# A two-layer latent attention network on one core: the heads' outputs scaled by ScalarE, one activation per head, and the statistics of the context rows placed anew

## The chip, the cores and the metric

The kernel runs on 1 core of one Trainium2 chip. The metric is the device time of one execution in microseconds (us), as a median of runs: 2179.64 us of 3 (2179.64 to 2184.43).

## The reference

`x` is 16 batches of 64 latents of width 128, `ctx` 16 batches of 1601 context rows of width 128. Six blocks add to `x`, one after the other: a cross attention (16 heads of 64), a selective scan, a small attention with a mixture of experts, a second cross attention (with a mask over the context), a state space block, and a feed-forward block with 4-bit quantization. The change touches the two cross attentions, which are, cut to what matters:

```python
xn = layer_norm(ctx); lat = layer_norm(x)
q = lat @ Wq
kv = concatenate([xn, lat], axis=1) @ Wkv            # 1601 + 64 rows
logits = einsum('bhld,bhsd->bhls', q * scale, k * scale)
w = softmax(logits, axis=-1)                         # in the second one masked
out = einsum('bhls,bhsd->bhld', w, v)
x = x + out.transpose(0, 2, 1, 3).reshape(b, 64, 1024) @ Wo
```

The kernel never makes k and v: the head weights are folded into the queries (`qk_hi`, `qk_lo`) and into an output matrix per head (`vo_c` for context rows, `vo_l` for latents), and a column of ones yields the softmax's sum.

## The kernel before, in words

One function, `cross_attention` (L120), prepares weights and calls `attention_loop` (L497), once unmasked (the first loop) and once masked (the second loop). The loop goes over the 16 batches, in pairs: `par` is 0 for the first batch of a pair and 1 for the second. One batch is called a half (of a pair). The engines run their own programs, and meet only through semaphores. Pair 0, pair 6 and pair 7 are written out; pairs 1 to 5 are five trips of a hardware loop (`Fori`, L665), so that each engine jumps back four times per attention, at the end of a `par` 1 half.

A half is 28 steps u (26 for 13 tiles of 128 context rows by two groups of 8 heads, 2 for the latents). In step u:

- TensorE (L875 on) makes the scores of step u + 3 (three matmuls, L786 to L788), into a ring of 4 PSUM banks, then the products of step u with the context rows (three matmuls, L805 to L807), then the side items of the step. Scores of u + 3 need the ring place that `p_lo` of step u - 1 frees. In the last steps the first scores of the next half are made: two of them in step 26, one in step 27. Before the products of step 26 it waits until the bank pair `aux` is free.
- ScalarE (L936 on) makes two exponentials of each score tile: `p_hi` in fp16 (L929), then the same in fp32 in place (L930). After these of step u it works on the side items of step u - 1 (`LAG` is 1). At the end of a half it copies the sums out of PSUM (L943), once the products of step 25 are done, and then takes the next half's step 0.
- VectorE (L1129 on) makes `p_lo`, the rest (L1134), then parts of the statistics of context rows (first loop only), then the side items of step u - 1. In step 1 it copies the latents' sums of the half before out of `aux` (L1099).
- GpSimd normalizes context rows (L264) and splits them into fp16 halves (L221, L223) in the first loop, splits queries of the second batch of a pair (L962, L952, at the end of a `par` 1 half), and adds up the heads' outputs (`add_heads`, L709).
- SyncE issues the DMAs: rows that carry the maxima (L729, L731), raw context rows (L179 on), stores and transposed loads.

Side items share the PSUM bank pair `aux`, so each waits until the one before is read (semaphore `aux_free`). `items` (L572) places them: 16 `max` items (the row maxima of the next batch's scores) and a `turn` in each half, four `q` items at the start of a `par` 1 half, and in a `par` 0 half three `out` items at steps 20, 21 and 22: outputs of the pair before for 6, 6 and 4 heads, each head two fp32 matmuls of 129 columns (L812, L813). VectorE's `project` (L1101) takes an `out` item: reciprocals of the sums (L1113, two instructions of 3 heads), then products of outputs and reciprocals (L1119, two instructions), which free `aux`. Seven `par` 0 halves of each attention have `out` items (all but the first).

The statistics (`context_stats`, L227) of one batch are 13 `bn_stats` (L236), an aggregation of five small instructions (L243 to L249), an addition (L253) and nine dependent steps of a reciprocal square root. Before, those for batch b + 2 run in half b: four `bn_stats` in each of steps 0 to 2, one in step 3, the rest in steps 3 to 8. GpSimd's L264 waits for them.

Of the kernel before, what the change touches and what calls it, by code (L numbers as in the profile page):

```python
# [14 lines left out]
ACT = mybir.ActivationFunctionType  # L15
# [3 lines left out]
B, L, D = 16, 64, 128  # L19
# [45 lines left out]
STATS_PARTS = 4 + 2 + RSQRT_STEPS  # L65
# [54 lines left out]
def cross_attention(nc, glob, name, ctx_dram, mask_dram, w_dram):  # L120
# [12 lines left out]
    with ExitStack() as st:  # L133
# [93 lines left out]
        def context_stats(v, wait, n, par, i, part):  # L227


            if part == 0:  # L230
                x_step[0] = Steps(v, norm_steps, n * NORM_STEPS)
                v.wait_ge(raw_in[par], (i + 1) * 48)
            steps = x_step[0]
            if part < 4:
                for j in range(4 * part, min(4 * part + 4, KT)):
                    steps.mark(v.bn_stats(xstats[:, j, :], raw[par][:, j, :]))  # L236
            elif part == 4:
# [12 lines left out]
            else:  # L250
                steps.wait()
                if part == 5:
                    steps.mark(v.tensor_scalar(xrv[:, :], xvar[:, :], LN_EPS, None, ALU.add))  # L253
                else:
                    steps.mark(rsqrt_step(v, part - 6, xr[:, :], xrv[:, :], xrt[:, :]))
# [16 lines left out]
        with ExitStack() as pre:  # L272
# [53 lines left out]
            def copy_of(n, made):  # L326
# [6 lines left out]
                (VF_C, 0, range(0, 4)), (VF_L, 0, range(4, 8)), (K_C, 0, range(8, STATS_PARTS)), (VO + 2, 1, range(0, 4)))}  # L333
# [163 lines left out]
def attention_loop(nc, glob, name, st, sb, sem, psum, held, mask_dram, context_stats, context_normal):  # L497
# [74 lines left out]
    def items(par, first, last, pre=False):  # L572
# [14 lines left out]
        for item in todo:  # L587
# [3 lines left out]
            else:  # L591
                u += 1 + {paused: PAUSE[par][0], ("max", 2 * NC_ - 1): PAUSE[par][1]}.get(item, 0)
# [118 lines left out]
    with nc.Block() as block:  # L711
        @block.sync
        def _(sp):
# [32 lines left out]
            def body(at):  # L746
# [3 lines left out]
                if at.has_next:  # L750
                    rows(at)
                if at.has_next3 and not masked:
                    sp.wait_ge(xt_ready, at.b + 2)
                    load_raw(sp, at.b + 3, at.npar, at.ni + 1)
                if at.has_next2:
# [288 lines left out]
        def _(v):  # L1044
            def stats_parts(u):

                if u < 4:
                    return (u,), (4,) if u == 3 else ()
                parts = [k for k in (2 * u - 3, 2 * u - 2) if k < STATS_PARTS]
                return parts[:1], parts[1:]  # L1050
# [50 lines left out]
            def project(a, at, ready, pair, used=None):  # L1101
# [3 lines left out]
                if a == 0 and used is not None:  # L1105
                    v.wait_ge(later_q_used, used)
                if a == 0 and not (isinstance(pair, int) and pair == 0):
                    v.wait_ge(sum_steps, pair * SUM_STEPS)
# [5 lines left out]
                steps.wait()  # L1114
# [7 lines left out]
            def before(at):  # L1122
                for item in at.index:
                    consume(at, item)
                    if item == ("q", Q_ITEMS - 1) and not masked:
                        for part in range(4, STATS_PARTS):
                            context_stats(v, wait_alone, 1, 1, 0, part)

            def body(at):  # L1129
                for u in range(STEPS):  # L1130
# [6 lines left out]
                    soon, later = stats_parts(u) if at.has_next2 and not masked else ((), ())  # L1137
                    for part in soon:
# [1267 lines left out]
```

## Time and profile before

| what | value |
|---|---|
| median of 3 runs | 2179.64 us |
| profiled execution | 2175.95 us, its span 2174.3 us |
| TensorE busy | 2012.8 us, 93% |
| VectorE busy | 1700.0 us, 78% |
| ScalarE busy | 1284.3 us, 59% |
| first attention loop | about 90 to 906 us of the span |
| second attention loop | about 1221 to 2002 us of the span |

Busy times are shares of the whole span over stages with different limits; inside the loops the rows of the timeline tell which engine is waited for. A span of several instructions in one row ("x2") runs from the first one's start to the last one's end. An ACT or DVE instruction's shown duration overlaps with the next one's start.

### The profile page before, as it was taken

To read this page: it belongs to the slowest core of one execution; us is meant where nothing else is said; L and a number is where in the kernel's file an instruction comes from. 1 tells how busy PE (TensorE), PEld (TensorE's weight loads), DVE (VectorE), ACT (ScalarE), POOL (GpSimd) and SP (SyncE) were. 2 spreads that over 40 slices of the span, in tenths; PEclk is the share of its full clock that TensorE was granted. 3 is DMA by queue.
4 is the path that set the end of the run, shared out by engine and by line. 5 is a ranking of instruction groups with operands and counts; after the bars stand their busy time and mean duration, and the time that the engine had idled before them with its cause. 6 is when DMAs were issued, how large, how long until landed. Compare 5 with 4: busy or idle time off the path is not lost. (4 is left out here: it accounts for less than half of the span.)

```text
span 2174.3 us, 37348 instructions
## 1 busy us (share of the span) xinstructions
PE 2012.8 (93%) x11706; PEld 1090.7 (50%) x11706; DVE 1700.0 (78%) x4108; ACT 1284.3 (59%) x2308; POOL 600.7 (28%) x648
## 2 busy tenths in 40 slices
PE   5899999999999999889798999999999999999886
PEld 4444545353535455433567445454545454544584
DVE  5789797979788887589666877778787979785657
ACT  2376666666666666644323486868687777777211
POOL 3435353534343432059201102121111111110000
PEclk8899999999999999989999899999999999999897
DMA  3222222222222211033104012121111111110100
GB/s 111 81 64 64 65 64 63 64 63 63 63 64 63 91 37 48 9 95 126 48 1 110 5 37 52 31 61 36 35 36 36 36 36 37 36 33 1 27 2 10
DMA packets 148169, 108.91 MB, mean 50 GB/s; under 512 B 120748, under 2 KB 136088, under 8 KB 148024
## 3 DMA queue, kind: packets, MB, share of 16 engines
q1 hardware_dynamic: 148024, 107.26, 17.2%
q8 instruction: 57, 0.93, 0.2%
q14 instruction: 88, 0.72, 0.1%
HBM read 65.15 MB, written 14.29 MB: 37 GB/s over the span
## 5 line engine op out<-in xcount | busy, mean ns | idle before, releaser
L1134 DVE TENSOR_TENSOR x_p_lo<-x_psum,x_p_hi 128x512 f16<-128x512 f32 (+2 forms) x896 | 605.5, 684 | 153.8 <-ACT x_psum L930 141.1
L929 ACT ACTIVATE x_p_hi<-x_psum 128x512 f16<-128x512 f32 (+2 forms) x480 | 287.4, 599 | 303.3 <-PE x_psum L788 301.5
L929 ACT ACTIVATE x_p_hi<-x_psum,x_bcol 128x512 f16<-128x512 f32 (+1 forms) x416 | 288.8, 694 | 139.6 <-PE x_psum L788 137.4
L805 PE MATMUL x_psum<-x_p_hi,x_x_both 128*128 128x512 f16 (+1 forms) x832 | 316.7, 381 | 33.1 <-DVE x_p_lo L1134 32.5
L786 PE MATMUL x_psum<-x_q,x_xT_both 128*128 128x512 f16 x832 | 316.9, 381 | 0.9 <-DMA x_q<-x_shift_rows 0.7
L807 PE MATMUL x_psum<-x_p_hi,x_x_both 128*128 128x512 f16 (+1 forms) x832 | 315.8, 380 | 0.0
L787 PE MATMUL x_psum<-x_q,x_xT_both 128*128 128x512 f16 x832 | 315.8, 380 | 0.0
L806 PE MATMUL x_psum<-x_p_lo,x_x_both 128*128 128x512 f16 (+1 forms) x832 | 315.8, 380 | 0.0
L788 PE MATMUL x_psum<-x_q,x_xT_both 128*128 128x512 f16 x832 | 315.8, 380 | 0.0
L1073 DVE CUSTOM_DVE_ANT_0 x_junk<-x_psum,x_brow 128x512 bf16<-128x512 f32 (+2 forms) x512 | 279.7, 585 | 9.9 <-PE x_psum L852 9.2
L930 ACT ACTIVATE x_psum<-x_psum 128x512 f32<-128x512 f32 (+2 forms) x480 | 286.0, 596 | 0.6
L852 PE MATMUL x_psum<-x_xT_both,x_q 128*128 128x512 f16 (+2 forms) x1024 | 268.9, 340 | 15.0 <-DVE x_mx L1076 3.9
L1076 DVE TENSOR_REDUCE x_mx<-x_psum 128x1 f32<-128x512 f32 (+2 forms) x512 | 276.5, 585 | 6.9 <-PE x_psum L852 6.4
L930 ACT ACTIVATE x_psum<-x_psum,x_bcol 128x512 f32<-128x512 f32 (+1 forms) x416 | 276.2, 664 | 0.2
L264 POOL TENSOR_SCALAR x_xt<-x_raw,x_xmean,x_xr 128x127 f32<-128x127 f32 x208 | 166.5, 816 | 298.1 <-DVE x_xr L85 298.1
L852 PEld LDWEIGHTS x_psum<-x_xT_both,x_q 128*128 128x128 f16 x1024 | 99.0, 97 | 186.7 <-DVE x_mx L1076 48.6
L979 POOL TENSOR_SCALAR x_brow<-x_mrow 128x1536 bf16<-128x1536 uint8 x16 | 36.3, 2266 | 531.6 <-DVE x_shift_rows L1095 479.2
L805 PEld LDWEIGHTS x_psum<-x_p_hi,x_x_both 128*128 128x128 f16 (+1 forms) x832 | 81.0, 97 | 171.7 <-DVE x_p_lo L1134 85.3
L709 POOL TENSOR_TENSOR x_prod<-x_prod 128x1024 f32<-128x1024 f32 (+3 forms) x56 | 67.0, 1197 | 237.1 <-DVE x_prod L1119 233.8
L788 PEld LDWEIGHTS x_psum<-x_q,x_xT_both 128*128 128x128 f16 x832 | 81.4, 98 | 98.6 <-issue 0.3
L807 PEld LDWEIGHTS x_psum<-x_p_hi,x_x_both 128*128 128x128 f16 (+1 forms) x832 | 81.4, 98 | 98.4 <-issue 0.3
L806 PEld LDWEIGHTS x_psum<-x_p_lo,x_x_both 128*128 128x128 f16 (+1 forms) x832 | 81.5, 98 | 79.5 <-issue 0.3
(450 smaller groups left out, 3256.9 us busy)
## 6 DMA issues: line engine op xcount, KB each, us to landing
x_x_both<-context_rows SPq DMA_DIRECT2D x32, 832.0 KB, 5.4
context_rows<-x_x SPq DMA_DIRECT2D x16, 832.0 KB, 5.7
x_raw<-in_ctx SPq DMA_DIRECT2D x16, 768.0 KB
ssm_c_row<-ssm_bc_rows SPq DMA_DIRECT2D x16, 512.0 KB, 4.1
ssm_b_wide<-ssm_bc_rows SPq DMA_DIRECT2D x7, 512.0 KB, 3.5
x_mrow<-in_mask_BxS_bk SPq DMA_DIRECT2D x16, 200.1 KB
x_Wkv<-in_L_xattn_Wkv SPq DMA_DIRECT2D x4, 512.0 KB, 4.9
x_xT_both<-context_rows SPq DMA_TRANSPOSE x96, 3.7
```

Source lines behind the costliest of these rows:

```text
L786: pe.matmul(out, k_hi, q_hi[s][par][:, chunks, :], start=True, stop=False)
L787: pe.matmul(out, k_hi, q_lo[s][par][:, chunks, :], start=False, stop=False)
L788: pe.matmul(out, k_lo, q_hi[s][par][:, chunks, :], start=False, stop=True).then_inc(s_ready, 1)
L805: pe.matmul(out, v_hi, p_hi[r][rows, :], start=start, stop=False)
L806: pe.matmul(out, v_hi, p_lo[r][rows, :], start=False, stop=False)
L807: pe.matmul(out, v_lo, p_hi[r][rows, :], start=False, stop=stop).then_inc(pv_done, 1)
L852: ins = pe.matmul(aux[:, 512 * bank:512 * bank + w], lhs, xT_hi[at.npar][:, k:k + w], start=True, stop=True)
L929: act.activation(p_hi[r][rows, :], score[r][rows, :], ACT.Exp, scale=SCORE_UNIT, **bias).then_inc(p_hi_ready, 1)
L930: act.activation(score[r][rows, :], score[r][rows, :], ACT.Exp, scale=SCORE_UNIT, **bias).then_inc(p32_ready, 1)
L1073: ins = v.tensor_tensor_reduce(junk[:, 512 * bank:512 * bank + w], src, brow[:, w0:w0 + w], 1.0, -3.4e38, ALU.add, ALU.max, m)
L1076: ins = v.tensor_reduce(m, src, AX.X, ALU.max)
L1134: v.tensor_tensor(p_lo[r][rows, :], score[r][rows, :], p_hi[r][rows, :], ALU.subtract).then_inc(p_lo_ready, 1)
```

## The change

It has four parts. In both loops, VectorE's `project` keeps only the reciprocals; the products move to ScalarE as one activation (copy with the reciprocal as a per-partition scale) per head, 6, 6 and 4 of them, taken as side items at step u - 1 = 20, 22 and 24. The `out` items get a free step behind the first and the second, so that they stand at steps 20, 22 and 24. In the first loop, the `bn_stats` and the aggregation for batch b + 3 run in steps 23 to 27 of half b (3, 3, 3, 2, 2 and then the aggregation), and the reciprocal square root of that batch in steps 0 to 3 of the next half (3, 2, 3, 1). The first half keeps its early statistics too. And SyncE issues the load of raw rows ahead of the maxima's rows and no longer behind them. After the loop, VectorE scales the last pair's outputs itself (`scale_last`).

```diff
+STATS_OF = ((0, 3), (3, 6), (6, 9), (9, 11), (11, KT))
+AGGR = len(STATS_OF)
+ROOTS = AGGR + 2
+STATS_PARTS = ROOTS + RSQRT_STEPS
...
-                u += 1 + {paused: PAUSE[par][0], ("max", 2 * NC_ - 1): PAUSE[par][1]}.get(item, 0)
+                u += 1 + {paused: PAUSE[par][0], ("max", 2 * NC_ - 1): PAUSE[par][1], ("out", 0): 1, ("out", 1): 1}.get(item, 0)
...
-                if at.has_next:
-                    rows(at)
                 if at.has_next3 and not masked:
                     sp.wait_ge(xt_ready, at.b + 2)
                     load_raw(sp, at.b + 3, at.npar, at.ni + 1)
+                if at.has_next:
+                    rows(at)
...
                 kind, a = item
+                if kind == "out":
+
+                    if a == 0:
+                        act.wait_ge(later_q_used, LATER_PARTS * (at.i + 1))
+                    act.wait_ge(out_steps, (at.i - 1) * OUT_STEPS + 2 * (a + 1))
+                    for j, h in enumerate(out_heads(a)):
+                        ins = act.activation(prod[:, h, :], out_place(j, aux)[:, 0:D], ACT.Copy, scale=rec[:, h:h + 1])
+                    ins.then_inc(aux_free, 2)
+                    return
...
-            def stats_parts(u):
-
-                if u < 4:
-                    return (u,), (4,) if u == 3 else ()
-                parts = [k for k in (2 * u - 3, 2 * u - 2) if k < STATS_PARTS]
-                return parts[:1], parts[1:]
+            def stats_parts(u, at):
+
+                if at.first and at.par == 0:
+                    early = [[k] for k in range(AGGR)] + [[AGGR, AGGR + 1]]
+                    early += [[k, k + 1, k + 2] for k in range(ROOTS, STATS_PARTS, 3)]
+                else:
+                    early = [[ROOTS, ROOTS + 1, ROOTS + 2], [ROOTS + 3, ROOTS + 4], [ROOTS + 5, ROOTS + 6, ROOTS + 7], [ROOTS + 8]]
+                late = {LAST - AGGR + 1 + k: [k] for k in range(AGGR)}
+                late[LAST] += [AGGR, AGGR + 1]
+                return early[u] if u < len(early) else (), late.get(u, ())
...
-                steps.wait()
+
+            def scale_last(a, at):
+                v.wait_ge(out_steps, (PAIRS - 1) * OUT_STEPS + 2 * (a + 1))
+                if a == 0:
+                    v.wait_ge(sum_steps, (PAIRS - 1) * SUM_STEPS)
+                heads = out_heads(a)
                 for g in range(0, len(heads), 3):
...
-                    soon, later = stats_parts(u) if at.has_next2 and not masked else ((), ())
-                    for part in soon:
+                    two, three = stats_parts(u, at) if not masked else ((), ())
+                    for part in two if at.has_next2 else ():
                         context_stats(v, wait_alone, at.b + 2, at.par, at.i + 1, part)
                     for item in at.items.get(u - LAG, []):
                         if item[0] == "out":
-                            project(item[1], aux, at.ready(item), at.i - 1, LATER_PARTS * (at.i + 1))
+                            project(item[1], aux, at.ready(item), at.i - 1)
                         else:
                             consume(at, item)
-                    for part in later:
-                        context_stats(v, wait_alone, at.b + 2, at.par, at.i + 1, part)
+                    for part in three if at.has_next3 else ():
+                        context_stats(v, wait_alone, at.b + 3, at.npar, at.ni + 1, part)
```

## Rows read from the trace of the kernel before

**Rows 1.** The page's first part: engine, busy us, share, instructions.
```profile
PE 2012.8 (93%) x11706; PEld 1090.7 (50%) x11706; DVE 1700.0 (78%) x4108; ACT 1284.3 (59%) x2308; POOL 600.7 (28%) x648
```
**Rows 2.** Timeline of PE: start, us, line, count [idle before].
```profile
544.82 0.39 PE L812 MATMUL x_psum<-x_vo_c,x_sum_c 128*128 128x129 f32 x2
...
547.50 0.38 PE L786 MATMUL x_psum<-x_q,x_xT_both 128*128 128x512 f16 x1
...
549.26 0.49 PE L812 MATMUL x_psum<-x_vo_c,x_sum_c 128*128 128x129 f32 x2 [0.31 <-DVE x_prod L1119]
...
553.61 0.49 PE L812 MATMUL x_psum<-x_vo_c,x_sum_c 128*128 128x129 f32 x2
...
555.50 0.38 PE L786 MATMUL x_psum<-x_q,x_latTphi 128*128 128x512 f16 x1
...
564.98 0.22 PE L832 MATMUL x_psum<-x_lnT_hi,x_qk_hi 128*128 x1
...
1567.36 0.22 PE L832 MATMUL x_psum<-x_lnT_hi,x_qk_hi 128*128 x1
```
**Rows 3.** Timeline of DVE in the same `par` 0 half.
```profile
547.91 0.25 DVE L1113 RECIPROCAL x_rec<-x_psum 128x3 f32<-128x3 f32 x2 [2.29 <-PE x_psum L813]
548.19 1.02 DVE L1119 TENSOR_TENSOR x_prod<-x_psum,x_rec 128x384 f32<-128x384 f32 x2
549.13 0.68 DVE L1134 TENSOR_TENSOR x_p_lo<-x_psum,x_p_hi 128x512 f16<-128x512 f32 x1
...
561.03 0.69 DVE L1134 TENSOR_TENSOR x_p_lo<-x_psum,x_p_hi 128x512 f16<-128x512 f32 x1 [1.61 <-ACT x_psum L930]
```
**Rows 4.** Timeline of ACT in the same `par` 0 half.
```profile
542.51 0.60 ACT L929 ACTIVATE x_p_hi<-x_psum 128x512 f16<-128x512 f32 x1 [1.43 <-PE x_psum L788]
...
548.35 0.59 ACT L929 ACTIVATE x_p_hi<-x_psum 65x512 f16<-65x512 f32 x1 [2.89 <-PE x_psum L788]
548.84 0.58 ACT L930 ACTIVATE x_psum<-x_psum 65x512 f32<-65x512 f32 x1
...
558.93 1.08 ACT L943 ACTIVATE x_sum_c<-x_psum 128x512 f32<-128x512 f32 x2 [0.23 <-PE x_psum L807]
```
**Rows 5.** Groups of ACT by form: count | busy us, mean ns.
```profile
L929 ACT ACTIVATE x_p_hi<-x_psum,x_bcol 128x512 f16<-128x512 f32 x384 | 267.0, 695 | 91.8 <-PE x_psum L788 89.8
...
L929 ACT ACTIVATE x_p_hi<-x_psum 128x512 f16<-128x512 f32 x384 | 230.6, 601 | 202.3 <-PE x_psum L788 202.3
...
L2305 ACT ACTIVATE fp_hT<-fp_psum 96x128 f32<-96x128 f32 x8 | 2.1, 268 | 0.0
```
**Rows 6.** Waits: who for whom, us in total, times, longest.
```profile
PEld x_psum L812 <- DVE x_prod L1119: 18.7, 28, 0.8
```
**Rows 7.** Timeline of DVE: a jump back of the loop, a written-out boundary.
```profile
500.49 2.60 DVE L1134 TENSOR_TENSOR x_p_lo<-x_psum,x_p_hi 65x512 f16<-65x512 f32 x4
506.87 0.69 DVE L1134 TENSOR_TENSOR x_p_lo<-x_psum,x_p_hi 128x512 f16<-128x512 f32 x1 [3.78 <-ACT x_psum L930]
...
515.08 0.69 DVE L1134 TENSOR_TENSOR x_p_lo<-x_psum,x_p_hi 128x512 f16<-128x512 f32 x1
...
819.68 0.69 DVE L1134 TENSOR_TENSOR x_p_lo<-x_psum,x_p_hi 128x512 f16<-128x512 f32 x1 [1.85 <-ACT x_psum L930]
```
**Rows 8.** Groups of DVE in the half of 508 to 562 us.
```profile
L236 DVE BATCH_NORM_STATS2 x_xstats<-x_raw 128x6 f32<-128x128 f32 x13 | 2.9, 277 | 0.0
```
**Rows 9.** Line L1081: duration ns min/median/max, first and last start.
```profile
L1081 DVE TENSOR_TENSOR x_shift<-x_const_rows x32: 400/407/1802, 80.5 to 1944.2; 8x256 f32<-8x256 f16 x32
```
**Rows 10.** Timeline of DVE: L1081 in a `par` 0 half.
```profile
538.55 1.79 DVE L1081 TENSOR_TENSOR x_shift<-x_const_rows 8x256 f32<-8x256 f16 x1
```
**Rows 11.** Timeline of POOL.
```profile
503.62 4.49 POOL L952 TENSOR_TENSOR x_q<-x_prod,x_q 128x512 f16<-128x512 f32 x4
...
536.73 3.34 POOL L223 TENSOR_TENSOR x_x<-x_xt,x_x 128x1664 f16<-128x1664 f32 x1 [0.15 <-POOL x_x L221]
```

More of the change, by code:

```diff
@@ L64 @@
 NORM_STEPS = KT + 5 + 1 + RSQRT_STEPS
-STATS_PARTS = 4 + 2 + RSQRT_STEPS
+STATS_OF = ((0, 3), (3, 6), (6, 9), (9, 11), (11, KT))
+AGGR = len(STATS_OF)
+ROOTS = AGGR + 2
+STATS_PARTS = ROOTS + RSQRT_STEPS
 def rsqrt_step(v, k, out, val, t):
@@ L232, in context_stats @@
                 v.wait_ge(raw_in[par], (i + 1) * 48)
+            if part == ROOTS:
+                x_step[0] = Steps(v, norm_steps, n * NORM_STEPS)
+                x_step[0].n = KT + 5 + 1
             steps = x_step[0]
-            if part < 4:
-                for j in range(4 * part, min(4 * part + 4, KT)):
+            if part < AGGR:
+                for j in range(*STATS_OF[part]):
                     steps.mark(v.bn_stats(xstats[:, j, :], raw[par][:, j, :]))
-            elif part == 4:
+            elif part == AGGR:
                 if not (isinstance(n, int) and n == 0):
@@ L251, in context_stats @@
                 steps.wait()
-                if part == 5:
+                if part == AGGR + 1:
                     steps.mark(v.tensor_scalar(xrv[:, :], xvar[:, :], LN_EPS, None, ALU.add))
                 else:
-                    steps.mark(rsqrt_step(v, part - 6, xr[:, :], xrv[:, :], xrt[:, :]))
+                    steps.mark(rsqrt_step(v, part - ROOTS, xr[:, :], xrv[:, :], xrt[:, :]))
             assert part < STATS_PARTS - 1 or steps.n == NORM_STEPS
@@ L332, in cross_attention @@
             STATS_WITH = {n: [(b, part) for part in parts] for n, b, parts in (
-                (VF_C, 0, range(0, 4)), (VF_L, 0, range(4, 8)), (K_C, 0, range(8, STATS_PARTS)), (VO + 2, 1, range(0, 4)))}
+                (VF_C, 0, range(0, AGGR)), (VF_L, 0, range(AGGR, ROOTS + 2)), (K_C, 0, range(ROOTS + 2, STATS_PARTS)), (VO + 2, 1, range(0, AGGR)))}
             if masked:
@@ L1099, in latents_sums, with project @@
                 v.tensor_copy(sum_l[:, :, par, :], aux.rearrange("p (h l) -> p h l", l=L)).then_inc(aux_free, 2)
-            def project(a, at, ready, pair, used=None):
+            def project(a, at, ready, pair):
                 steps = Steps(v, out_steps, pair * OUT_STEPS + 2 * a)
                 v.wait_ge(aux_ready, ready)
[L1105 to L1108, printed above, removed]
                 heads = out_heads(a)
@@ L1125, in before @@
                     if item == ("q", Q_ITEMS - 1) and not masked:
-                        for part in range(4, STATS_PARTS):
+                        for part in range(AGGR, STATS_PARTS):
                             context_stats(v, wait_alone, 1, 1, 0, part)
@@ L1152, in _ @@
                 project(a, last_place(a), 2 * (k + a + 1 - B), PAIRS - 1)
+                scale_last(a, last_place(a))
             v.wait_ge(aux_free, 2 * (k + OUT_ITEMS))
```

## The prediction

> **What bounds the kernel now.** I read the page's first part, then the table of waits, then the timelines of TensorE, VectorE and ScalarE side by side over one `par` 0 half of the first loop (508 to 562 us) and one of the second, then the jump back of the loop. TensorE is busy 93% of the span, so it is the engine to feed; ScalarE with 59% looks as if it had room for more [rows 1]. In the steps with `out` items TensorE works through 12 fp32 matmuls in 2.68 us (544.82 to 547.50) for six heads and in 1.89 us (553.61 to 555.50) for four [rows 2]. VectorE and ScalarE wait there, not TensorE: VectorE 2.29 us before the reciprocals [rows 3], ScalarE 2.89 us before exponential 24 [rows 4]. TensorE waits for the scaling only before the second and third item, 18.7 us of weight loads' idle time in all, 28 times [rows 6].
>
> The reader is to see one more thing in rows 4. ScalarE ran exponential 22 at 542.51, long before the first `out` item was made. It is ahead of VectorE, and that lead is what keeps the chain short: when VectorE is done with the scaling at 549.1, `p_lo` 22 starts at once [rows 3].
>
> **Part 1, the scaling moves.** VectorE loses two products an item, six a pair: 1.02 us for an item of six heads [rows 3], some 2.8 us a pair. ScalarE gets 16 activations a pair. An activation's price here: 128 columns last 268 ns, 512 columns 601 ns, and with a per-partition pointer (the bias) 695, so 94 more [rows 5]. The trace has no 128-column one with a pointer. Two of 512 columns start 0.49 us apart (548.35, 548.84) though each lasts 0.59, so about 0.10 of each is hidden [rows 4]. My value: 0.268 + 0.094 - 0.10, 0.27 us each when back to back (an estimate), so 1.6 for six heads and 1.1 for four. Ends: 0.17 (the pointer costs nothing) and 0.36 (nothing overlaps).
>
> What counts is the order on ScalarE. It takes the item of step 20 after the exponentials of step 21, and then waits in order: exponentials 22 and 23, which it made early before, stand behind the wait for the reciprocals. VectorE's `p_lo` 22 waits for exponential 22, and TensorE's products 22 wait for `p_lo` 22. Before: reciprocals, scaling, `p_lo`. Now: reciprocals, scaling, two exponentials, `p_lo`. And the free step behind each item takes away what TensorE did meanwhile: `out` 1 ran at 549.26, ahead of products 22.
>
> I walk it in the profiled half, with: three fp16 matmuls 0.65; matmuls' end to reciprocals 0.20 (0.41 the first time) and 0.25 for them [rows 2, 3]; 0.1 to ScalarE (estimate); from the start of a pair of exponentials 1.10 to `p_lo` (0.49 + 0.58 + 0.03) and 0.98 to ScalarE's next instruction [rows 4]; `p_lo` 0.68 [rows 3].
>
> - `out` 0 ends 547.50; reciprocals until 548.16; ScalarE scales until 549.91; `p_lo` 22 at 551.01 (549.13 before). TensorE had finished products 21 and scores 25 at 549.45, and starts products 22 at 551.74: 2.3 us idle. `out` 1 runs 552.39 to 555.07.
> - Products 23 and scores 26 and 27 fill TensorE to 557.02. Reciprocals until 555.52, scaling until 557.27, exponential 24, `p_lo` 24 at 558.37, products 24 at 559.10: 2.1 us idle. `out` 2 runs 559.75 to 561.64.
> - Products 25 and two sets of next scores fill until 563.59. Scaling until 563.29, exponential 26, `p_lo` 26 at 564.39, products 26 at 565.12: 1.5 us idle. `aux` is free in time.
> - ScalarE goes on without a gap: exponential 27 at 564.27, sums' copies 1.0 [rows 4], exponential 0 of the next half at 566.23. `p_lo` 0 at 567.33, before at 561.03 [rows 3].
> - In step 1 of the next half VectorE frees `aux` (L1099) at about 570.3, and only then does TensorE start `q` 0: 570.35, before at 564.98 [rows 2].
>
> So the half gets 5.4 us longer, with TensorE's old waits for the scaling already gone from the count. In the second loop the exponentials with a bias pointer last 94 ns more [rows 5], with four such pairs in the chain, and the same walk ends 5.9 us later than the 1567.36 of before [rows 2]. From `q` 0 on TensorE is the bound in both, so I see nothing that gives it back. Seven such halves in each loop: 7 x 5.4 + 7 x 5.9 = 79 us. With 0.17 or 0.36 for an activation the chain of 16 is 1.6 shorter or 1.4 longer: 57 to 99.
>
> **Part 2, the statistics.** At the jump back VectorE is idle 3.78 us, at a boundary without one 1.85 [rows 7]. The jump follows its last instruction, and that is now later by 13 `bn_stats` (2.9 us, [rows 8], less the overlap, 2.5) and six small ones (about 1.0, an estimate from two reciprocals in 0.25, [rows 3]): 3.6 us. In the next three steps 12 `bn_stats` go (2.3) and eight roots at about 0.2 come (1.6): so the fifth `p_lo` (515.08, [rows 7]) is late by 2.9. Four jumps: +11.6. At the written-out boundaries, and at the ends of `par` 0 halves, VectorE's idle time hides the added work: 0. What is won: L1081 takes 0.41 usually and 1.8 in the `par` 0 halves of the first loop whose statistics run (one of eight such in [rows 10]; median and maximum in [rows 9]). There it ends as GpSimd's L223 ends, 536.73 + 3.34 = 540.07 [rows 11]. With the roots done at step 3 instead of 8, GpSimd is through some 8 us before, in six halves (the first keeps its early order): -6 x 1.39 = -8.3. Sum +3.3, with ends -8 (nothing lost at the jumps) and +11.6 - 8.3 + 4 x 4.5 = +21: the aggregation falls in the time of GpSimd's L952 (4.49 us, [rows 11]), and each small instruction could wait as L1081 did.
>
> The Trainium skill's GPSIMD Engine Reference, section Specifications, says that GpSimd's SBUF interface is shared with VectorE and is contended by VectorE instructions with two SBUF inputs; the long L1081 (two SBUF inputs) agrees, and by that rule the aggregation's subtraction and addition would wait too, 1 us or so per jump, which lies inside the bounds above.
>
> **Part 3, SyncE.** The raw load is issued at the start of a half instead of between the maxima's rows and the store; three issues less stand before the store, 1.6 us. VectorE is late there by more than that, so 0; ends 0 and -1.6 x 6 = -10.
>
> **Sum.** 79 + 3 = 82. The profiled execution took 2175.95, 3.7 less than the median of 2179.64. 2175.95 + 82 = 2258, against the median 2262.
>
> **The rivals.**
>
> - Faster: ScalarE's lead hides it all. If it reached the items with its exponentials done (as VectorE's did), the moved work would fall into 2.9 us of its idle time, TensorE would lose its waits before L812 in 14 halves (about -10 of the 18.7 us of [rows 6], since a weight load's idle time is partly hidden), and L1081's stall would go (-8.3): 2161. It decides at whether exponential u + 2 stands before or behind item u on ScalarE. The diff puts it behind. 7%.
> - Half of it: the activations are cheap (0.17), handovers shorter, and something later in the half absorbs 1.5 us of the shift: 14 x 3.3 = 46, about 2226. For it: the waits before L812 are short, 0.7 each [rows 6], so handovers here are quick. Against: TensorE has no idle time from `q` 0 to the `turn`. 13%.
> - More: the small VectorE instructions wait for GpSimd at jumps and also where L709 runs now, at the start of `par` 1: 2262 + 18 + 7 x 1 = 2287. 12%.
> - ScalarE's jump back. Now VectorE alone pays for it [rows 7]; with 16 more activations and their waits in a trip ScalarE could pay the same 3.8 us at 8 jumps, +30: 2292. For it, VectorE's trip is longer than ScalarE's, against it, it stays shorter after the change too. 3%. The Trainium skill (Runtime: NRT & Kernel Launch, Instruction fetch mechanics) says that a taken branch whose target is out of a two-page window waits for a fetch; VectorE's 3.78 us fit that, and of ScalarE's room no row tells.
> - The change is hidden: 5%, 2180.
>
> The forecast has 60%. A difference under 0.3% (6.5 us) could not be told from none. Faster 0.07, same 0.05, slower 0.88. Range: from 2222 to 2290, which leaves out the first and last rival and some of the fourth.
>
> **What would show it.** Right: in a `par` 0 half ScalarE is idle some 7 us behind exponential 21, until the reciprocals are there, then six activations, then L929; TensorE idle about 2.3, 2.1 and 1.5 us before L805, released by `p_lo`, and no more at L812; halves of the second loop with `out` items 6 us longer, `par` 1 halves the same; L1081 at 0.41 from the third half on; VectorE's idle time at the jump still near 3.8, but starting 3.6 later. Wrong: exponential 22 before the first scaling, or `par` 0 halves of the second loop within 1 us of their length before.

## The result, and the profile after

The changed kernel takes 2279.14 us (median of 4, 2278.13 to 2280.14) against 2180.77 for the kernel before in the same runs: 4.5% slower, ratio 1.0448 [1.043, 1.0466]. The profiled execution took 2280.1 us. Forecast: 2262, range 2222 to 2290. The measured difference is 98.4 us, the forecast one was 82.

Names after: scores L792 to L794, products L811 to L813, `out` L818 and L819, exponentials L944 and L945, ScalarE's scaling L919, reciprocals L1128, `p_lo` L1154, shift addition L1100 (was L1081), sums' copies L958 and L1118, `bn_stats` L242, aggregation L249 to L259.

The page's first part, which answers to [rows 1]: 10 us left VectorE, 53 came to ScalarE, and the span of the profiled execution grew by 104.

```profile
PE 2030.2 (89%) x11706; PEld 1106.2 (49%) x11706; DVE 1690.2 (74%) x4024; ACT 1337.0 (59%) x2532; POOL 601.7 (26%) x648
```

The page's groups (count | busy us, mean ns of one | idle time ahead of them, what ended most of it). ScalarE's 224 activations sit behind 167.5 us of waiting for reciprocals. TensorE's products have 107.3 us of idle time that `p_lo` ended. The weight loads' waits for the scaling, 18.7 us in [rows 6], are gone.

```profile
L1154 DVE TENSOR_TENSOR x_p_lo<-x_psum,x_p_hi 128x512 f16<-128x512 f32 (+2 forms) x896 | 609.1, 684 | 249.9 <-ACT x_psum L945 225.8
L811 PE MATMUL x_psum<-x_p_hi,x_x_both 128*128 128x512 f16 (+1 forms) x832 | 319.1, 384 | 108.6 <-DVE x_p_lo L1154 107.3
L919 ACT ACTIVATE x_prod<-x_psum,x_rec 128x128 f32<-128x128 f32 x224 | 62.5, 374 | 167.5 <-DVE x_rec L1128 167.5
```

The table of waits (us in total, times, longest) for TensorE's products, first of the kernel before, then of the changed one, shows where the new time went:

```profile
PE x_psum L805 <- DVE x_p_lo L1134: 32.5, 49, 1.5
```

```profile
PE x_psum L811 <- DVE x_p_lo L1154: 123.9, 92, 6.3
```

ScalarE's timeline in a `par` 0 half of the first loop (start, us, line, count [idle before]); it answers to [rows 4]. Exponential 21 ends at 457.66, and the next thing is the first item, 5.52 us later. Exponentials 22 and 23 (464.69 on) stand behind it, where before exponential 22 ran ahead of the item. The same happens before the second and the third item.

```profile
457.07 0.59 ACT L945 ACTIVATE x_psum<-x_psum 128x512 f32<-128x512 f32 x1
463.18 1.66 ACT L919 ACTIVATE x_prod<-x_psum,x_rec 128x128 f32<-128x128 f32 x6 [5.52 <-DVE x_rec L1128]
464.69 0.63 ACT L944 ACTIVATE x_p_hi<-x_psum 128x512 f16<-128x512 f32 x1
...
470.41 1.66 ACT L919 ACTIVATE x_prod<-x_psum,x_rec 128x128 f32<-128x128 f32 x6 [3.60 <-DVE x_rec L1128]
...
476.71 1.14 ACT L919 ACTIVATE x_prod<-x_psum,x_rec 128x128 f32<-128x128 f32 x4 [2.69 <-DVE x_rec L1128]
```

VectorE in the same stretch, answering to [rows 3]: from reciprocals to `p_lo` 22 it was 1.2 us (547.91 to 549.13), now it is 2.95, and VectorE is idle for 2.70 of it.

```profile
462.89 0.25 DVE L1128 RECIPROCAL x_rec<-x_psum 128x3 f32<-128x3 f32 x2 [2.08 <-PE x_psum L819]
465.84 0.69 DVE L1154 TENSOR_TENSOR x_p_lo<-x_psum,x_p_hi 128x512 f16<-128x512 f32 x1 [2.70 <-ACT x_psum L945]
```

TensorE, at products 22, 24 and 26 of that half. In the fifth half of the second loop the same three rows read 1.95, 1.92 and 1.21.

```profile
466.59 0.39 PE L811 MATMUL x_psum<-x_p_hi,x_x_both 128*128 128x512 f16 x1 [1.79 <-DVE x_p_lo L1154]
...
473.80 0.39 PE L811 MATMUL x_psum<-x_p_hi,x_x_both 65*128 65x512 f16 x1 [1.76 <-DVE x_p_lo L1154]
...
479.57 0.39 PE L811 MATMUL x_psum<-x_p_hi,x_latphi 64*128 64x512 f16 x1 [1.22 <-DVE x_p_lo L1154]
```

The second thing to see is the jump back. VectorE's timeline, answering to [rows 7]: the aggregation's L249 and L250 take 0.96 and 1.19 us (0.17 each in the kernel before, where GpSimd is idle), the last small instruction ends at 535.66, and `p_lo` 0 comes 4.29 us later, with nothing to wait for ("issue"). L249 and L250 end at 533.62 and 534.73, each as one of GpSimd's four L967 ends (533.58 and 534.70).

```profile
532.66 0.96 DVE L249 TENSOR_TENSOR x_xd<-x_xstats 128x13 f32<-128x13 f32 x1
533.54 1.19 DVE L250 TENSOR_TENSOR x_xm<-x_xstats 128x13 f32<-128x13 f32 x1
...
535.45 0.21 DVE L259 TENSOR_SCALAR x_xrv<-x_xvar 128x13 f32<-128x13 f32 x1
539.96 0.69 DVE L1154 TENSOR_TENSOR x_p_lo<-x_psum,x_p_hi 128x512 f16<-128x512 f32 x1 [4.29 <-issue]
```

GpSimd in that stretch works on the queries (as in [rows 11], 4.5 us):

```profile
530.19 4.51 POOL L967 TENSOR_TENSOR x_q<-x_prod,x_q 128x512 f16<-128x512 f32 x4
```

TensorE's first products behind the jump, of the kernel before and then of the changed one: 0.76 us idle became 6.22. At the four jumps of the first loop it is 1.22, 1.22, 0.76 and 1.24 before, and 6.29, 6.14, 6.22 and 6.21 after.

```profile
507.79 0.39 PE L805 MATMUL x_psum<-x_p_hi,x_x_both 128*128 128x512 f16 x1 [0.76 <-DVE x_p_lo L1134]
```

```profile
540.88 0.60 PE L811 MATMUL x_psum<-x_p_hi,x_x_both 128*128 128x512 f16 x1 [6.22 <-DVE x_p_lo L1154]
```

And the same jump of the changed kernel by windows (the number behind POOL's count is the granted TensorE clock, then the DMA share and GB/s). From 536 to 539 no engine works. From 539 on TensorE runs at 0.50, its 1.2 GHz level, for 6.8 us; this happens behind all four jumps (near 307, 423, 539 and 655 us). Before, windows over the same jump show 1.00 throughout, and no stretch at the lower clock follows any of the first loop's jumps.

```profile
536.00:539.00 3.00, 0.00 (x0) 0.00 (x0) 0.00 (x0) 0.00 (x0) 0.00 (x0) 1.00 1.04 229
539.00:541.00 2.00, 0.12 (x1) 0.13 (x2) 0.97 (x4) 0.00 (x0) 0.00 (x0) 0.52 0.97 319
541.00:543.00 2.00, 2.00 (x6) 0.62 (x6) 1.98 (x4) 0.00 (x0) 0.00 (x0) 0.50 0.93 376
```

What was won, answering to [rows 9]: the shift addition's longest is 1106 ns, no longer 1802. The 1106 is the one at 82.5 us, ahead of the loop. Of the seven that took 1.73 to 1.80 us in the first loop's `par` 0 halves, the first now takes 0.69 and the others 0.40.

```profile
L1100 DVE TENSOR_TENSOR x_shift<-x_const_rows x32: 402/406/1106, 82.5 to 2043.2; 8x256 f32<-8x256 f16 x32
```

### The profile page after: what moved, and what is told of

It is laid out like the page before. It is cut to its first block and busy times, and to the rows that moved or that the text cites. A ratio compares the mean times of both kernels' runs of the same rounds, so it can differ in the third digit from the quotient of the medians.

```text
span 2278.3 us, 37473 instructions
## 1 busy us (share of the span) xinstructions
PE 2030.2 (89%) x11706; PEld 1106.2 (49%) x11706; DVE 1690.2 (74%) x4024; ACT 1337.0 (59%) x2532; POOL 601.7 (26%) x648
## 5 line engine op out<-in xcount | busy, mean ns | idle before, releaser
L1154 DVE TENSOR_TENSOR x_p_lo<-x_psum,x_p_hi 128x512 f16<-128x512 f32 (+2 forms) x896 | 609.1, 684 | 249.9 <-ACT x_psum L945 225.8
L944 ACT ACTIVATE x_p_hi<-x_psum 128x512 f16<-128x512 f32 (+2 forms) x480 | 288.1, 600 | 224.7 <-PE x_psum L794 221.9
L811 PE MATMUL x_psum<-x_p_hi,x_x_both 128*128 128x512 f16 (+1 forms) x832 | 319.1, 384 | 108.6 <-DVE x_p_lo L1154 107.3
L944 ACT ACTIVATE x_p_hi<-x_psum,x_bcol 128x512 f16<-128x512 f32 (+1 forms) x416 | 290.0, 697 | 92.2 <-PE x_psum L794 90.8
L792 PE MATMUL x_psum<-x_q,x_xT_both 128*128 128x512 f16 x832 | 318.5, 383 | 1.2 <-DMA x_q<-x_shift_rows 1.1
L813 PE MATMUL x_psum<-x_p_hi,x_x_both 128*128 128x512 f16 (+1 forms) x832 | 317.8, 382 | 0.0
L794 PE MATMUL x_psum<-x_q,x_xT_both 128*128 128x512 f16 x832 | 316.8, 381 | 0.0
L945 ACT ACTIVATE x_psum<-x_psum 128x512 f32<-128x512 f32 (+2 forms) x480 | 287.2, 598 | 0.6
L945 ACT ACTIVATE x_psum<-x_psum,x_bcol 128x512 f32<-128x512 f32 (+1 forms) x416 | 277.5, 667 | 0.2
L858 PE MATMUL x_psum<-x_xT_both,x_q 128*128 128x512 f16 (+2 forms) x1024 | 263.5, 338 | 12.0 <-DVE x_mx L1095 4.5
L811 PEld LDWEIGHTS x_psum<-x_p_hi,x_x_both 128*128 128x128 f16 (+1 forms) x832 | 81.4, 98 | 252.2 <-DVE x_p_lo L1154 140.5
L919 ACT ACTIVATE x_prod<-x_psum,x_rec 128x128 f32<-128x128 f32 x224 | 62.5, 374 | 167.5 <-DVE x_rec L1128 167.5
L813 PEld LDWEIGHTS x_psum<-x_p_hi,x_x_both 128*128 128x128 f16 (+1 forms) x832 | 81.9, 98 | 100.0 <-issue 3.0
L794 PEld LDWEIGHTS x_psum<-x_q,x_xT_both 128*128 128x128 f16 x832 | 81.7, 98 | 99.8 <-issue 2.4
```

Of the source, the lines that this page charges most:

```text
L792: pe.matmul(out, k_hi, q_hi[s][par][:, chunks, :], start=True, stop=False)
L794: pe.matmul(out, k_lo, q_hi[s][par][:, chunks, :], start=False, stop=True).then_inc(s_ready, 1)
L811: pe.matmul(out, v_hi, p_hi[r][rows, :], start=start, stop=False)
L813: pe.matmul(out, v_lo, p_hi[r][rows, :], start=False, stop=stop).then_inc(pv_done, 1)
L858: ins = pe.matmul(aux[:, 512 * bank:512 * bank + w], lhs, xT_hi[at.npar][:, k:k + w], start=True, stop=True)
L944: act.activation(p_hi[r][rows, :], score[r][rows, :], ACT.Exp, scale=SCORE_UNIT, **bias).then_inc(p_hi_ready, 1)
```

## The experiments

Eleven runs. The two loop columns are measured in the profiled execution, from the first half's `p_lo` 0 to the last half's, in us.

| run | median | ratio to before, 95% | loop 1 | loop 2 |
|---|---|---|---|---|
| before | 2180.77 | | 780.0 | 745.2 |
| after | 2279.14 | 1.0448 [1.043, 1.0466] | 838.3 | 785.4 |
| act_only | 2265.9 | 1.0403 [1.0386, 1.042] | 819.1 | 786.9 |
| act_nospace | 2241.0 | 1.0289 [1.0266, 1.0313] | 806.1 | 779.4 |
| dve_scale | 2212.8 | 1.0159 [1.0142, 1.0176] | 812.4 | 743.2 |
| late | 2204.06 | 1.0122 [1.0105, 1.0139] | 808.2 | 740.0 |
| stats_only | 2198.72 | 1.0089 [1.0073, 1.0106] | 798.7 | 744.7 |
| late_old | 2173.6 | 0.9972 [0.996, 0.9983] | 775.3 | 741.6 |
| agg_next | 2167.22 | 0.994 [0.9924, 0.9957] | 771.6 | 739.9 |
| late_roots | 2164.6 | 0.9932 [0.9912, 0.9952] | 769.5 | 741.5 |
| late_flat | 2178.84 | 1.0004 [0.9993, 1.0015] | 784.9 | 739.4 |
| agg_pad | 2176.92 | 0.9988 [0.9974, 1.0003] | 771.5 | 749.6 |
| roots_flat | 2157.49 | 0.9911 [0.9882, 0.994] | 765.4 | 739.4 |

The kernel before took 2178.98 beside the runs from act_only to late, 2179.92 beside those from stats_only to late_roots, and 2178.51 beside the last three.

**act_only**: the kernel before with the scaling on ScalarE and the free steps; statistics and SyncE's order as they were.

```diff
+                if kind == "out":
...
+                        ins = act.activation(prod[:, h, :], out_place(j, aux)[:, 0:D], ACT.Copy, scale=rec[:, h:h + 1])
```

> The kernel before with only the move to ScalarE and the free steps behind the out items; statistics and SyncE order as before. Theory A (the loss comes from the order on ScalarE, and the jumps of the loop from the statistics): the second loop's growth of 40 us is all of this kind, and the first loop's out halves grow by 5.4 to 6.1 each; 2181 + 40 + 38 to 43 = 2259 to 2264. Theory B (the statistics in steps 23 to 27 and the out items hinder one another, so the loss needs both): the second loop still +40, but the first loop's share of the out items well below 38, time 2220 to 2240.

Measured: +86.9 us, +39.1 in the first loop and +41.7 in the second. The moved scaling with its free steps carries most of the loss, and costs about the same in both loops.

**act_nospace**: act_only without the free steps.

```diff
-                u += 1 + {paused: PAUSE[par][0], ("max", 2 * NC_ - 1): PAUSE[par][1], ("out", 0): 1, ("out", 1): 1}.get(item, 0)
+                u += 1 + {paused: PAUSE[par][0], ("max", 2 * NC_ - 1): PAUSE[par][1]}.get(item, 0)
```

> As the one with only the move to ScalarE, but the out items at steps 20, 21, 22 as before. Theory A with its walk: the scaling of item 20 ends at 549.9, out 1 starts at once instead of after products 22, so TensorE has work while exponential 22 and p_lo 22 run; products 26 end about 3.1 us later than before instead of 5: 14 x 3.1 = 43, 2181 + 43 = 2224. If the free steps matter nothing: 2260. If the loss is the price of 16 small activations alone, the same 2260.

Measured: 62 us over before, 25 less than act_only. So the free steps add 25 us, and the other 62 come with the move itself. My walk for this case said 2224, 17 too little. Part of that is in the second loop's `par` 1 halves, which I had not walked: they got 1.1 us longer than before (51.6 against 50.5).

**dve_scale**: the changed kernel with the products back on VectorE; free steps, statistics and SyncE as changed.

```diff
-                    for j, h in enumerate(out_heads(a)):
-                        ins = act.activation(prod[:, h, :], out_place(j, aux)[:, 0:D], ACT.Copy, scale=rec[:, h:h + 1])
...
+                            scale(item[1], aux, at.i - 1, LATER_PARTS * (at.i + 1))
```

> The changed kernel with the products back on VectorE (two of three heads at most per item, behind the reciprocals); free steps, statistics and SyncE order kept. Theory A: the second loop is back near the kernel before (free steps cost a few tenths per half: p_lo 22 at 549.1 while TensorE has nothing after 549.45; and save the waits for aux), so within -8 to +8 there; the first loop keeps the jumps' +5.6 x 4 less 1.9 x 6, about +13. 2181 + 13 = 2194 (2186 to 2202). If the statistics were the main loss: above 2220.

Measured: 2212.8, 34 us slower than before, where 13 to 15 were expected. All of it is in the first loop (+32.4), so the second loop shows that free steps alone cost nothing (743.2 against 745.2). The statistics' price was mis-sized.

**late**: the changed kernel, but ScalarE takes item u behind the exponentials of step u + 3, and no longer behind those of u + 1.

```diff
+                    for item in at.items.get(u - AHEAD, []):
+                        if item[0] == "out":
+                            parts(at, item)
...
-                        parts(at, item)
+                        if item[0] != "out":
+                            parts(at, item)
```

> The changed kernel, but ScalarE takes an out item of step u after the exponentials of step u + 3 instead of u + 1 (their scores are made before the item); the 16 activations and all else stay. Theory A: exponentials 22 and 23 run early again, p_lo 22 follows the reciprocals at once, so the idle 2.3, 2.1 and 1.5 us go, and the halves with out items shrink by 5 to 6.5: 2279 - 14 x 6 = 2195, perhaps 10 less, as VectorE has no products in its way. Rival (what costs is that ScalarE does the work at all, its 374 ns per activation or their reads of PSUM): it stays within 15 of 2279.

Measured: 2204.06, where 2195 was expected: 75 us faster than the changed kernel with the same number of activations on the same engine, and the second loop (740.0) is 5 us shorter than before. VectorE's timeline of `late`: the two `p_lo` follow the reciprocals without a gap, where the changed kernel had 2.70 us.

```profile
449.30 0.25 DVE L1132 RECIPROCAL x_rec<-x_psum 128x3 f32<-128x3 f32 x2 [2.08 <-PE x_psum L819]
449.46 1.26 DVE L1158 TENSOR_TENSOR x_p_lo<-x_psum,x_p_hi 128x512 f16<-128x512 f32 x2
```

ScalarE of `late`: the item comes behind 2.52 us of idle time, with exponential 23 (446.47) already made.

```profile
446.47 0.59 ACT L945 ACTIVATE x_psum<-x_psum 128x512 f32<-128x512 f32 x1
449.58 1.66 ACT L919 ACTIVATE x_prod<-x_psum,x_rec 128x128 f32<-128x128 f32 x6 [2.52 <-DVE x_rec L1132]
```

**stats_only**: the kernel before with the statistics and SyncE's order of the change; scaling on VectorE, no free steps. The diff is the change's own in `STATS_OF`, `stats_parts` and `load_raw`.

> The kernel before with the statistics placed as in the change and SyncE's order of the change; products on VectorE at steps 20, 21, 22 as before. The second loop must be that of before (745 us over 15 halves). My prediction's working gave +3 for the first loop, the runs so far +19 on top of the move and +32 with the free steps. Theory A (the late statistics cost at the jump back, 6 us each for four, and behind the out items at the end of par 0 halves): +25 to +35 without the move, 2179 + 30 = 2209. Theory B (they cost only together with the free steps, which leave VectorE idle where it now has bn_stats): +3 to +12, 2187.

Measured: +18.8 us, all in the first loop. It lies between the two theories. By halves, counted from `p_lo` 0 to the next half's `p_lo` 0: the four that end in a jump went from 51.5 to 56.8 us (+21), the two that end in a written-out boundary from 49.2 to 53.4 and 52.6 (+8), and the `par` 0 halves got 10 us shorter together, 5.7 of it in the first one with `out` items (57.5 to 51.8). So the rest of dve_scale's 32 comes of free steps and placement together: there the `par` 0 halves last 55 us instead of 53, and L249 at their ends takes 1.16 us instead of 0.18. With the free steps the aggregation meets GpSimd there too.

**late_old**: the kernel before with late activations and free steps, statistics as before (act_only with the edit of `late`).

> The kernel before with the activations on ScalarE behind exponentials u + 3 and the free steps, but old statistics and SyncE order. Theory A: the second loop is 5 us shorter than before (740), as in the run with the late activations, and the first loop as much or a little more (VectorE without 2.8 us of products a pair): 2179 - 5 - 6 = 2168. Rival (the second loop's gain came from something that in the first VectorE's statistics hide): 2174 or more.

Measured: 2173.6, 6.3 us faster than before (0.28%), where 2168 was expected; the median alone stands nearer to the rival's 2174. The loops are 4.7 and 3.6 us shorter. The moved scaling, in this order, is at best a small gain, and in the other a loss of 87: its sign hung on where it stands in ScalarE's order.

**agg_next**: `late`, with the aggregation moved from the last step into step 0 of the next half; the nine roots follow in steps 1 to 3.

```diff
-                    early = [[ROOTS, ROOTS + 1, ROOTS + 2], [ROOTS + 3, ROOTS + 4], [ROOTS + 5, ROOTS + 6, ROOTS + 7], [ROOTS + 8]]
+                    early = [[AGGR, AGGR + 1]] + [[k, k + 1, k + 2] for k in range(ROOTS, STATS_PARTS, 3)]
...
-                late[LAST] += [AGGR, AGGR + 1]
```

> The kernel with the late activations, and the aggregation (six small VectorE instructions) moved from step 27 to step 0 of the next half, where GpSimd's L952 (two inputs, fp16 out) is over; roots in steps 1 to 3. Theory: at each jump the aggregation takes 3.0 us instead of about 1.0 because its instructions wait for GpSimd; away from there it takes 1.0, and the jump starts 3.0 earlier: the first p_lo behind it comes after 5.6 instead of 8.6, the aggregation's 1.0 comes back in step 0: 4 x -2 = -8, and as much or less at the ends of par 0 halves, where L709 runs: 2204 - 8 to - 16 = 2188 to 2196. Rival (the 3 us are the chain of waits itself): -0 to -3, 2202.

Measured: 37 us faster than `late`, all in the first loop, where 8 to 16 were expected. The halves that end in a jump give 18 of it, those before a written-out boundary 3, the `par` 0 halves 15. VectorE's timeline at a jump of `agg_next`: `p_lo` 0 comes 1.24 us after the last instruction of the trip, and L249 comes behind it and takes 0.33.

```profile
501.21 0.69 DVE L1157 TENSOR_TENSOR x_p_lo<-x_psum,x_p_hi 64x512 f16<-64x512 f32 x1
501.94 0.49 DVE L242 BATCH_NORM_STATS2 x_xstats<-x_raw 128x6 f32<-128x128 f32 x2
503.67 0.69 DVE L1157 TENSOR_TENSOR x_p_lo<-x_psum,x_p_hi 128x512 f16<-128x512 f32 x1 [1.24 <-ACT x_psum L945]
504.28 0.33 DVE L249 TENSOR_TENSOR x_xd<-x_xstats 128x13 f32<-128x13 f32 x1
```

The pause is still there, and where it starts is what changed. The trace also has the records of VectorE's sequencer, which takes the loop's branch; the timeline leaves them out. The new trip's first record (a register update of the loop's line, L671) stands 0.11 us ahead of `p_lo` 0 in both kernels:

| | last `p_lo` starts | branch | VectorE's last instruction ends | new trip's first record | `p_lo` 0 |
|---|---|---|---|---|---|
| before | 502.40 | 502.45 | 503.09 | 506.76 | 506.87 |
| after | 531.34 | 535.54 | 535.66 | 539.85 | 539.96 |
| agg_next | 501.21 | 500.79 | 502.43 | 503.56 | 503.67 |

In agg_next the branch is 0.42 us ahead of the last `p_lo`, with 1.64 us of VectorE's work still to run; in the changed kernel it comes 4.20 us behind that `p_lo`, with 0.12 us left to run. In the kernel's text nothing in the last step of agg_next waits for VectorE's own results, while the aggregation waits for them several times. From the branch to the new trip's first record it is 2.8 to 3.4 us at the four jumps, against 4.2 to 4.3 in the changed kernel and 4.3 to 4.8 before. At this jump the earlier branch is worth 4.6 us and the shorter pause 1.5. Why the pause is shorter no run shows. The exponential to which the view puts the wait had ended 0.23 us before `p_lo` 0.

**late_roots**: late_old with the nine roots in steps 4 to 6.

```diff
-                parts = [k for k in (2 * u - 3, 2 * u - 2) if k < STATS_PARTS]
-                return parts[:1], parts[1:]
+                parts = {4: [5, 6, 7, 8], 5: [9, 10, 11], 6: [12, 13, 14]}.get(u, [])
+                return parts[:2], parts[2:]
```

> As the one with late activations on the kernel before, and the nine root steps and the addition put into steps 4 to 6 instead of 3 to 8 (four, three, three). GpSimd's normalization starts some 3 to 4 us earlier, so L223 ends at about 536.5 in the profiled half, ahead of L1081 at 538.5. Theory: L1081 takes 0.4 instead of 1.8 in seven halves: -9 against the same kernel with the old roots, about 2159. Rival (the steps 4 to 6 get longer by what VectorE does there, and nothing gives that back): -3 or less, 2165.

Measured: 9 us faster than late_old, as the theory had it against the old roots; 5.8 us of it is in the profiled first loop. The shift addition of one half, in late_old and then in late_roots; the same step from 1.73 or 1.80 to 0.40 us shows in all seven `par` 0 halves that had it:

```profile
535.83 1.80 DVE L1094 TENSOR_TENSOR x_shift<-x_const_rows 8x256 f32<-8x256 f16 x1
```

```profile
530.56 0.40 DVE L1094 TENSOR_TENSOR x_shift<-x_const_rows 8x256 f32<-8x256 f16 x1
```

So the gain forecast for L1081 comes with earlier roots, without the statistics' new place.

**late_flat** and **roots_flat**: `late` and `late_roots` with the hardware loop written out, so that no engine jumps in the attentions.

```diff
-        with eng.Fori(1, PAIRS - 2) as i:
+        for i in range(1, PAIRS - 2):
```

> The kernel with the late activations, with the hardware loop of both attentions written out (pairs 1 to 5 as plain code). In the kernels so far VectorE passes 4.3 us between the loop's branch and its next instruction in the first loop and 3.5 in the second, ScalarE and GpSimd 0.26. Theory: that pause is what puts the late statistics of a par 1 half on the path; without a jump the first p_lo of the next half comes after 4.35 instead of 8.6 (as in the written-out pair 6 now): 4 x 4.2 + 4 x 1.0 = 21 less, 2183. Rival (code streaming costs as much everywhere, or p_lo waits for ScalarE anyway): 2198 or more.

> The best so far (late activations, free steps, roots in steps 4 to 6, old statistics and SyncE order), with the loops written out. There the first p_lo behind a jump comes after 4.7 in the first loop against 2.5 at written-out boundaries, 3.7 against 2.7 in the second: 4 x 2.2 + 4 x 1.0 = 13 less: 2165 - 13 = 2152. If the written-out code costs fetches elsewhere: 2160.

Measured: `late_flat` is 25 us faster than `late`, where 21 were expected. Behind a boundary `p_lo` 0 comes 4.37 us after the one before, where `late` has 8.5 to 8.7. Writing the loop out takes 23 us from the first loop of `late`, and 4 from that of `late_roots` (769.5 to 765.4), whose statistics are early. So about 19 us of what `late` loses there is the late statistics at the jumps. `roots_flat` is 7 us faster than `late_roots`, where 13 were expected, and has the lowest median, 2157.49, 0.9% under the kernel before. Its runs spread from 2150.79 to 2164.2 and the two intervals overlap, so the 7 us are not sure.

**agg_pad**: agg_next with twelve tiny memsets and one wait, executed once and ahead of the hardware loop's code.

```diff
+                    if not masked and at.first and at.par == 1 and u == 20:
+                        for k in range(12):
+                            v.memset(held["xd"][:, k:k + 1], 0.0).then_inc(padded, 1)
+                        v.wait_ge(padded, 12)
```

> The kernel with the aggregation in step 0, with 12 memsets of one column (and a wait for them) put once into step 20 of the half before the loop starts, so that the loop's code lies some 13 instructions further on, about where it lies in the kernel with the aggregation in step 27. In the former VectorE's pause behind the branch was 0.12 us, in the latter 4.3. Theory (the pause depends on where the loop's code lies): 4.3 again at four jumps, of which some 1 is hidden: 2167 + 12 = 2179. Rival (it depends on what stands before the branch, instructions that wait or not): pause stays 0.12, time 2167 to 2168.

Measured: 9.7 us slower than agg_next, near the number expected, but not in the expected place, so the number is luck. The first loop is the same to 0.1 us, and its pauses are those of agg_next (2.8 to 3.3 us from the branch to the new trip's first record). Both the theory and its rival started from a pause of 0.12 us in agg_next; that was no pause, but the distance from the branch to the trip's last `bn_stats`. What the first loop does show is the rival's point: what stands before the branch counts, and moving the code by 13 instructions does not. The second loop is 9.7 longer, in step 1 of the four `par` 0 halves that follow a jump. VectorE's timeline there, with the copy's idle time put down to the products L813:

```profile
1409.67 1.29 DVE L1161 TENSOR_TENSOR x_p_lo<-x_psum,x_p_hi 128x512 f16<-128x512 f32 x2 [3.02 <-issue]
1413.21 1.23 DVE L1121 COPY x_sum_l<-x_psum 128x1024 f32<-128x1024 f32 x1 [2.25 <-PE x_psum L813]
```

TensorE's timeline shows those products of the latents long done:

```profile
1409.49 0.38 PE L813 MATMUL x_psum<-x_p_hi,x_latplo 64*128 64x512 f16 x1
```

In agg_next the copy followed `p_lo` at once (1409.39). No engine holds it back for these 2.25 us, and the only edit is instructions that ran once, over 1200 us before. The DMA view has a queue that it calls "instruction". Asked for one of these four pauses alone (1512.5 to 1514.76), and then for the changed kernel's pause at a jump (535.66 to 539.96), it shows one packet in each:

```profile
q14 instruction: 1, 0.01, 0.9%
```

```profile
q14 instruction: 1, 0.01, 0.6%
```

The trace has the packets' times. In the four pauses of agg_pad one starts 1.8 to 2.0 us before the copy. At every jump back of every kernel here one starts between branch and new trip, 1.8 to 2.4 us before the new trip's first record. The queue has about 90 packets in a whole execution, so chance does not put one into each of these pauses. That VectorE waits for the loading of its instructions is thus shown by the times; the packets do not name the engine. So pauses stand also in straight code, and where they fall depends on where the code lies.

## Why the prediction was right, and where it was not

**Part 1, the order on ScalarE: right.** The walk's 2.3, 2.1 and 1.5 us of TensorE idle time were 1.8, 1.8 and 1.2, and ScalarE's idle time before the first item was 5.5 us, not some 7. The lengthening was sized well all the same: +5.4 and +5.9 us a half were predicted. In act_only the halves with `out` items and no stretch at the lower clock behind them are 5.2 to 5.6 us longer in the first loop and 5.8 to 6.1 in the second. Two things that the walk left out nearly cancel in the loops' +39.1 and +41.7, and that is luck: five of the 14 halves have such a stretch, and the `par` 1 halves, which were to stay the same, are up to 0.8 us shorter. An activation costs (464.69 - 463.18) / 6 = 0.25 us back to back, predicted 0.27; alone it lasts 374 ns, the 268 of [rows 5] plus 106, where I took 94. The rival that ScalarE's lead hides it all fell with the row at 463.18, and `late` shows that its condition was named rightly: with the exponentials ahead of the item the second loop is 5 us shorter than before.

In the changed kernel TensorE's clock fell to its lower level for 3.4 us in three of the 14 halves, each time behind an idle time of TensorE of 1.76, 1.91 or 1.95 us; such a half is 0.9 to about 2 us longer than its like.

**Part 2, the statistics: the step that failed.** Predicted +3.3, measured +18.8 alone (stats_only). Term by term:

- The fifth `p_lo` late by 2.9, four jumps: +11.6. Measured 56.8 - 51.5 = 5.3 a jump, +21. The six small instructions were put at 1.0 us together; at the jump they took 3.0 (532.66 to 535.66), of which GpSimd's work is about 1.5: in agg_next, where they meet the L971 of that kernel only at its end, the same six take 1.46 (504.28 to 505.74). "The jump follows its last instruction" was misread: before, the branch came 0.64 us ahead of the end of VectorE's last instruction, so part of the pause was covered, and behind the aggregation it is not. The pause itself did not grow: from the branch it was 4.3 to 4.8 us before, and is 4.2 to 4.3. The idle 3.78 that I read was the shortest of four (4.20, 4.24, 3.78, 4.27). And the work hidden behind the old pause was gone: before, ScalarE and TensorE had enough in hand to fill it but for 0.8 to 1.2 us; a later start of the same pause was 4.9 to 5.5 us more of TensorE's idle time, and behind it came 6.8 us at the lower clock.
- Written-out boundaries: 0. Measured 53.4 - 49.2 = 4.2 and 52.6 - 49.2 = 3.4 in stats_only. VectorE's idle 1.85 us there [rows 7] was less than the work added ahead of it: I booked cover without checking its size, though my own 3.6 us of added work is more than 1.85.
- L1081: -8.3. The shift addition went from 1.80 to 0.40 us, and in late_roots that was worth 5.8 us of the loop and 9 of the median. In stats_only the `par` 0 halves gave 10, but 5.7 in one that before waits 1.48 us for a transposed load and then runs at the lower clock (195.5 to 198.9 us), which I had not seen. The row of the kernel before:

```profile
195.41 0.88 PE L852 MATMUL x_psum<-x_xT_both,x_q 128*128 128x512 f16 x2 [1.48 <-DMA x_xT_both<-context_rows]
```

So +21 + 8 - 10 = 19, where the prediction had +11.6 + 0 - 8.3. Its upper end, +21, holds the 18.8, but by other terms: it put 4.5 us on each jump for GpSimd, which took about 1.5.

The Trainium skill's GPSIMD Engine Reference, section Specifications, names contention between GpSimd and VectorE instructions with two SBUF inputs. The prediction put that at 1 us or so a jump. The traces agree with the rule: L249 and L250 took 0.96 and 1.19 us beside GpSimd's L967 and 0.17 each in the kernel before, while `bn_stats`, with one input, stayed at 0.26 to 0.29.

**Part 3, SyncE: 0.** It wasn't tried alone. The wait for the transposed load that went in one half may be its doing or that of the late statistics. Roots in steps 4 to 6 alone don't remove it: it is 0.94 us in late_old and 0.97 in late_roots, which have SyncE's old order. This stays open, with at most those 5.7 us.

**The sum.** Predicted 79 + 3 = 82, measured 98.4 by the medians. In the profiled executions the second loop grew by 40.2 us (predicted 41) and the first by 58.3 (predicted 38 + 3), so the miss is in the first loop, and there in part 2. The medians of act_only and stats_only, +86.9 and +18.8, add up to 7 more than the whole change; in the profiled loops the two parts simply add: 39.1 + 18.7 = 57.8 against 58.3, and 41.7 - 0.5 = 41.2 against 40.2.

**The rivals.** The measured 2279 lies nearer to the rival "More" (2287) than to the forecast (2262). Half of that rival's condition holds: the small instructions do wait for GpSimd at the jumps, and with the free steps also at the ends of the `par` 0 halves. Its price does not: most of the miss is the uncovered pause and the boundaries, which no rival named. ScalarE's own jump stayed at 0.27 us, so that rival fell. One slip in the reading changes nothing in the sum: the 1.89 us for four heads are 8 fp32 matmuls, not 12.

## What to carry to other kernels

Where an engine that works in a fixed order runs ahead of the others, a moved instruction costs what stands behind it in that order, not its own duration: 224 activations of 0.25 us, 56 us in all, cost 87 us or gained 6 (act_only and late_old), by two steps of difference in where they stood. Before moving work to the end of a loop's trip, compare the pause at the jump with what the other engines still have in hand there. Keep chains that wait for the engine's own results out of the last step: the pause starts at the branch, and only work that the sequencer has already handed over covers it. This follows from the branch's place in three kernels, and no run varied it alone; agg_next, which moves such a chain, is 37 us faster than `late`. Behind a long idle time count TensorE's lower clock too. Small instructions with two SBUF inputs are cheap only while GpSimd is idle.

## What was unexpected of the hardware

- From VectorE's branch to the new trip's first record it was 3.4 to 3.7 us in the second loop of every kernel with a hardware loop, and 4.2 to 4.9 in the first, but for agg_next and agg_pad, where it was 2.8 to 3.4. ScalarE's was 0.24 to 0.27 in all.
- In agg_pad a pause of 2.2 to 2.5 us stood in straight code, four times. The Trainium skill (Runtime: NRT & Kernel Launch, Instruction fetch mechanics) says that straight code is prefetched in sequence, with the fetch hidden, and that a taken branch out of the two-page window waits for a fetch. The jumps agree with that. By the same rule agg_pad's second loop would have equalled agg_next's; it was 9.7 us longer, with an instruction packet in each of the four pauses, so here the fetch was not hidden in straight code.
- TensorE idle for 6.14 to 6.29 us was followed by 6.8 us at a granted clock of 0.50 at each of the changed kernel's four jumps of the first loop. In the kernel before, with 0.76 to 1.24 us idle there, it stayed at 1.00.
